# Reciprocals and products three to four slots later, room ahead of queries and post block, keys and scores at 112 columns

## What is computed

```python
# inputs: x (32, 56, 160), ctx_768 (32, 1500, 96); every weight is an input, fp32
def _L0_xattn_ref(hidden_states, encoder_hidden_states, w_q, w_k, w_v, w_k_dis, w_v_dis, w_out, b_out, n_heads):
    ...
    dis_tok = encoder_hidden_states[:, :N_AOE, :]
    anat_tok = encoder_hidden_states[:, N_AOE:N_AOE + N_IMG, :]
    delta_tok = encoder_hidden_states[:, -N_DELTA:, :]
    q = _heads(hidden_states @ w_q, n_heads)
    z_anat = _attend(q, _heads(anat_tok @ w_k, n_heads), _heads(anat_tok @ w_v, n_heads), scale)
    z_dis = _attend(q, _heads(dis_tok @ w_k_dis, n_heads), _heads(dis_tok @ w_v_dis, n_heads), scale)
    z_delta = _attend(q, _heads(delta_tok @ w_k_dis, n_heads), _heads(delta_tok @ w_v_dis, n_heads), scale)
    ...
    return out + residual

def cross_attention(x, ctx, wq, wk, wv, wo, bo):          # of L1: 20 heads of 64
    q = jnp.einsum('bne,ef->bnf', x, wq).reshape(B, N, HEADS, DHEAD).transpose(0, 2, 1, 3)
    k = jnp.einsum('bme,ef->bmf', ctx, wk).reshape(B, M, HEADS, DHEAD).transpose(0, 2, 1, 3)
    v = jnp.einsum('bme,ef->bmf', ctx, wv).reshape(B, M, HEADS, DHEAD).transpose(0, 2, 1, 3)
    scores = jnp.einsum('bhnd,bhmd->bhnm', q, k) * SCALE
    attn = jax.nn.softmax(scores, axis=-1)
    out = jnp.einsum('bhnm,bhmd->bhnd', attn, v)
    ...
    return jnp.einsum('bnf,fe->bne', out, wo) + bo

def block_forward(x, context, ...):                       # L1; L3 has the same form, 20 heads of 8
    x = cross_attention(layer_norm(x, g1, be1), layer_norm(x, g1, be1), wq1, wk1, wv1, wo1, bo1) + x
    x = cross_attention(layer_norm(x, g2, be2), context, wq2, wk2, wv2, wo2, bo2) + x
    return geglu_ff(layer_norm(x, g3, be3), w_ff1, b_ff1, w_ff2, b_ff2) + x

def _L2_xattn_ref(...):                                   # 8 heads of 20, last 4 context rows apart
    ...
    hs = _mha(query, keyt, valt)
    ca_hs1 = _mha(ca_q1, residual, residual)
    ...
    return out

x = _L0_xattn_ref(x, ctx_768, ...)
x = _L1_xattn_ref(x, ctx_768, ...)
x = _L2_xattn_ref(x, ctx_768, ...)
x = _L3_xattn_ref(x, ctx_768, ...)
```

## Time and profile before

| | us |
|---|---|
| median of 3 runs | 6163.31 (6159.48 to 6168.51) |
| the profiled execution, its own time | 6137.53 |
| its span in the profile | 6135.7 |
| TensorE busy | 5702.6 (93%) |
| TensorE weight loads busy | 4684.0 (76%) |
| VectorE busy | 2809.0 (46%) |
| ScalarE busy | 3107.8 (51%) |
| GpSimd busy | 3112.7 (51%) |
| mean granted clock of TensorE | 0.947 |

### The profile page before, as it was taken

How to read it: one execution, slowest core, us unless ns; L and a number is a source line. 1 busy time by engine, 2 the same in 40 slices (tenths; PEclk the granted TensorE clock), 3 DMA queues, 4 the chain that set the end, 5 groups by cost and what they waited for, 6 DMA issues and landing times.

```text
span 6135.7 us, 92602 instructions
## 1 busy us (share of the span) xinstructions
PE 5702.6 (93%) x34384; PEld 4684.0 (76%) x34384; DVE 2809.0 (46%) x5170; ACT 3107.8 (51%) x7280; POOL 3112.7 (51%) x3472
## 2 busy tenths in 40 slices
PE   7999999999999999988999999799999999999998
PEld 5777777778778877776666666588888878888887
DVE  1444444444444444434555555354444554444452
ACT  1445554545455545553445454256555555555554
POOL 0444444444444444463556555166555655555565
PEclk8899999999999999997899999599999999999998
DMA  2000000000000000000001011000000000000000
GB/s 55 12 16 16 16 13 15 16 16 15 16 15 12 13 16 11 16 20 19 27 24 32 25 29 41 8 19 16 18 16 15 20 18 19 16 15 18 15 19 10
DMA packets 84429, 114.48 MB, mean 19 GB/s; under 512 B 42814, under 2 KB 64682, under 8 KB 83978
## 3 DMA queue, kind: packets, MB, share of 16 engines
q1 hardware_dynamic: 83978, 108.56, 6.1%
HBM read 104.06 MB, written 4.46 MB: 18 GB/s over the span
## 4 chain that ended last, share of the span: by engine, by line
PE 68%; DVE 14%; ACT 8%; DMA 6%; issue 3%; POOL 2%; POOLq 0%; ACTq 0%; SPq 0%; DVEq 0%
PE ps_c L689 13%; PE ps_s L1128 6%; PE ps_c L1070 6%; PE ps_u L1143 5%; PE ps_s L1130 5%; PE ps_s L1129 5%; DVE mpiece L1452 5%; PE ps_u L1144 5%; PE ps_u L1145 5%; PE ps_c L1089 3%; ACT p L1819 2%; DMA w_area<-recs 2%; ACT p_hi L1821 2%; DMA sums<-uT 1%; DMA srec<-sums 1%
## 5 line engine op out<-in xcount | busy, mean ns | idle before, releaser
L1608 POOL TENSOR_TENSOR p_lo<-p,p_hi 125x448 fp32r<-125x448 f32 (+2 forms) x2688 | 2718.8, 1020 | 2292.3 <-ACT p_hi L1821 1626.0
L1819 ACT ACTIVATE p<-ps_s 125x448 f32<-125x448 f32 (+2 forms) x2688 | 1326.1, 493 | 2086.0 <-PE ps_s L1130 1903.5
L1821 ACT ACTIVATE p_hi<-ps_s 125x448 fp32r<-125x448 f32 (+2 forms) x2688 | 1316.0, 490 | 0.0
L1452 DVE TENSOR_REDUCE mpiece<-ps_c 125x1 f32<-125x500 f32 (+1 forms) x1984 | 1234.7, 668 | 105.2 <-PE ps_c L1070 98.2
L1128 PE MATMUL ps_s<-q_hi,ctxT_hi 105*125 105x448 f32 (+3 forms) x2688 | 1010.5, 376 | 38.1 <-ACT p_hi L1821 17.8
L1070 PE MATMUL ps_c<-ctxT_hi,q_hi 96*125 96x500 f32 (+1 forms) x2112 | 856.4, 432 | 132.6 <-DVE mpiece L1452 114.8
L1143 PE MATMUL ps_u<-p_hi,ctx_hi 125*97 125x448 f32 (+2 forms) x2688 | 975.9, 363 | 3.7 <-ACT uT L1809 2.7
L1129 PE MATMUL ps_s<-q_lo,ctxT_hi 96*125 96x448 f32 (+2 forms) x2688 | 934.8, 348 | 0.0
L1130 PE MATMUL ps_s<-q_hi,ctxT_lo 96*125 96x448 f32 (+2 forms) x2688 | 932.1, 347 | 0.0
L1144 PE MATMUL ps_u<-p_hi,ctx_lo 125*96 125x448 f32 (+2 forms) x2688 | 924.9, 344 | 0.0
L1145 PE MATMUL ps_u<-p_lo,ctx_hi 125*97 125x448 f32 (+2 forms) x2688 | 923.4, 344 | 0.0
(11 more groups left out here) (231 smaller groups left out, 6002.7 us busy)
## 6 DMA issues: line engine op xcount, KB each, us to landing
ctx_raw<-in_ctx SPq DMA_DIRECT2D x96, 562.5 KB
pT<-recs SPq DMA_DIRECT2D x32, 420.0 KB, 3.3
w_area<-recs SPq DMA_DIRECT2D x32, 420.0 KB, 3.2
w_area<-recs SPq DMA_DIRECT2D x32, 168.0 KB, 3.3
cs<-in_ctx SPq DMA_DIRECT2D x192, 6.0 KB, 3.0
x_between<-x_out SPq DMA_DIRECT2D x32, 80.0 KB
x_in<-x_between SPq DMA_DIRECT2D x32, 80.0 KB
w_area<-in_L_xattn_wq SPq DMA_DIRECT2D x2, 800.0 KB, 5.8
```

What stands on the lines that cost most here:

```text
L1452: z = V.tensor_reduce(mpiece[0:wide, k, r:r + 1], C(0, wide, n % banks(t), 0, PIECE), AX.X, ALU.max)
L1608: P.tensor_tensor(p_lo[0:kp, k % 3, 0:w], p32[0:kp, k % 2, 0:w], p_hi[0:kp, k % RING, 0:w].bitcast(F32), ALU.subtract).then_inc(*sig("pl_r ...
L1819: A(p32[0:kp, k % 2, 0:w], ps_s[0:kp, k % 2, 0:w], ACT.Exp, scale=DH[t.ph] ** -0.5)
L1821: A(p_hi[0:kp, k % RING, 0:w], ps_s[0:kp, k % 2, 0:w], ACT.Exp, scale=DH[t.ph] ** -0.5)\
```

## The change

It has four parts.

1. `normalise`: the reciprocals stand at slot 13 in place of 10. The products stand at POST-1 = 19 and then two slots apart (19, 21, 23), and four apart for b = 1 in phases 0 and 2 (19, 23, 27). In phase 1 there is one group of heads and one product, at 19. Before, they stood at 15, 16, 17.
2. `POST` is 20 in place of 16, so the second lane of phase 1 starts at slot 20 of 24. `TAIL` is 4 in place of 3. The `pre` laid ahead of a phase starts at slot 26 in place of 20.
3. `PARTS`: extra room ahead of `queries` (step 1) in all phases and ahead of `post` (step 1); and small extras in `pre` (steps 10, 27 and 30 in phase 0, step 13 in phase 2). As a half's slots stay as many, the other pieces move together.
4. In phase 0 the keys of the self attention (L862, L869) are computed at 2 x 56 columns in place of 2 x 64, as are its scores, and the two copies of the keys (VectorE L1301, ScalarE L1680) take 1120 columns in place of 1280. In phase 2 the scores (L1001) are computed at 56 columns a head. The queries keep their 64.

```diff
--- before.py
+++ after.py
@@ -391,13 +391,13 @@
 
 
         PARTS = {
-            "pre": ((40, 3, {4: 1, 7: 0.5, 8: 3, 10: 1, 14: 1.5, 16: 3, 18: 2, 22: 2, 27: 2, 30: 1, 34: 1, 35: 0.5, 37: 1,
-                             38: 1.5, 39: 2, 40: 4.5}), (29, 3.5, {5: 2, 15: 1.5, 22: 0.5, 23: 2}), (20, 2.5, {2: 3, 6: 1.5, 7: 0.5, 9: 2, 11: 0.5, 15: 1, 19: 2, 20: 1})),
-            "queries": ((7, 1, {7: 3}), (3, 3, {}), (7, 1, {7: 2})),
+            "pre": ((40, 3, {4: 1, 7: 0.5, 8: 3, 10: 1.5, 14: 1.5, 16: 3, 18: 2, 22: 2, 27: 2.5, 30: 1.5, 34: 1, 35: 0.5, 37: 1,
+                             38: 1.5, 39: 2, 40: 4.5}), (29, 3.5, {5: 2, 15: 1.5, 22: 0.5, 23: 2}), (20, 2.5, {2: 3, 6: 1.5, 7: 0.5, 9: 2, 11: 0.5, 13: 1, 15: 1, 19: 2, 20: 1})),
+            "queries": ((7, 1, {1: 2, 7: 3}), (3, 3, {1: 1}), (7, 1, {1: 2, 7: 2})),
             "split": ((4, 0.5, {}), (2, 0.5, {}), (4, 0.5, {})),
             "context": ((5, 1, {5: 6}), (4, 4, {}), (5, 1.5, {5: 3})),
             "maxima": ((31, 2.25, {}), (16, 3, {}), (31, 1.75, {})),
-            "post": ((15, 3, {6: 1, 14: 1}), (2, 1.5, {}), (15, 3, {6: 1.5})),
+            "post": ((15, 3, {1: 1, 6: 1, 14: 1}), (2, 1.5, {1: 1}), (15, 3, {1: 0.5, 6: 1.5})),
             "hand": ((1, 1, {}), (1, 1, {}), (1, 1, {})),
         }
 
@@ -405,8 +405,10 @@
         CUT = (18, 9, 3)
         LAST_NORM = (38, None, 18)
 
-        POST = 16
-        TAIL = 3
+        RECIP = 13
+        POST = 20
+        APART = (4, 2, 4)
+        TAIL = 4
 
         def schedule(eng, side, main):
 
@@ -528,7 +530,7 @@
                 elif not last:
                     lanes = [lane(before(t + 1, pre_b), 0.0, TAIL)]
                 elif t.ph < 2:
-                    lanes = [lane([part("pre", side.pre, At(t.ph + 1, 0, ahead=True))], POST + 4.0)]
+                    lanes = [lane([part("pre", side.pre, At(t.ph + 1, 0, ahead=True))], POST + 6.0)]
                 weave(main(t, 1, last=last), *lanes, apart(side.normalise(t, 0)))
 
             for ph in range(3):
@@ -857,8 +859,9 @@
                             if j == 0:
                                 pe.wait_ge(*(got("q_ready", t, 2) if w else got("ht_ready", t, 1)))
                                 pe.wait_ge(*late_loaded())
-                            z = both(C(0, 128, 0, 128 * j, 128), lambda i: l1_w[w][:, i, 128 * j:128 * j + 128],
-                                     lambda i: hT[:, i, :, :])
+                            each = slice(0, T if w else S)
+                            z = both(C(0, 128, 0, 128 * j, 128).rearrange("p (b s) -> p b s", b=2)[:, :, each],
+                                     lambda i: l1_w[w][:, i, 128 * j:128 * j + 128], lambda i: hT[:, i, :, each])
                         z.then_inc(*sig("qkv_psum"))
                     for b in range(2):
                         yield 24 + b
@@ -866,8 +869,8 @@
                             pe.wait_ge(*got("kb_ready", t, 2))
                             pe.wait_ge(*got("kb2_ready", t, 1))
                         for j in range(10):
-                            z = mm(C(S * b, S, 0, 128 * j, 128), qo3[:, j, S * b:S * b + S],
-                                   kb1[:, b, 2 * j:2 * j + 2, :], start=True, stop=True)
+                            z = mm(C(S * b, S, 0, 128 * j, 128).rearrange("p (e s) -> p e s", e=2)[:, :, 0:T],
+                                   qo3[:, j, S * b:S * b + S], kb1[:, b, 2 * j:2 * j + 2, 0:T], start=True, stop=True)
                     z.then_inc(*sig("s_psum"))
 
                     for b in range(2):
@@ -998,8 +1001,8 @@
                     pe.wait_ge(*got("vb_ready", t, 1))
                     for b in range(2):
                         for o, h0, h1 in ((0, 0, 8), (0, 8, 10), (1, 0, 6), (1, 6, 10)):
-                            z = mm(C(S * b, S, 0, 640 * o + S * h0, S * (h1 - h0)), q_small[:, o, b, :],
-                                   kb3[:, o, b, h0:h1, :], start=True, stop=True)
+                            z = mm(C(S * b, S, 0, 640 * o + S * h0, S * (h1 - h0)).rearrange("p (h s) -> p h s", s=S)[:, :, 0:T],
+                                   q_small[:, o, b, :], kb3[:, o, b, h0:h1, 0:T], start=True, stop=True)
                     z.then_inc(*sig("s_psum"))
                     yield 11
                     side.probs_T(t, 0, 10, 0)
@@ -1298,8 +1301,8 @@
                     side.norm(t, 0)
                     yield 23
                     dve.wait_ge(*got("qkv_psum", t, 3))
-                    V.tensor_copy(kb1[S:2 * S, :, 1::2, :].rearrange("p b j s -> p j b s"),
-                                  C(S, S, 0, 0, 1280).rearrange("p (j b s) -> p j b s", j=10, b=2))\
+                    V.tensor_copy(kb1[S:2 * S, :, 1::2, 0:T].rearrange("p b j s -> p j b s"),
+                                  C(S, S, 0, 0, 1280).rearrange("p (j b s) -> p j b s", j=10, b=2)[:, :, :, 0:T])\
                         .then_inc(*sig("kb_ready"))
                     yield 26
                     s = C(0, 128, 0, 0, 1280).rearrange("p (h w) -> p h w", h=20)[:, :, 0:T]
@@ -1468,11 +1471,11 @@
                 def normalise(t, b):
 
                     tiles = t.heads // 2
-                    yield 10
+                    yield RECIP
                     dve.wait_ge(*got("su_loaded", t, 16 * (b + 1)))
                     V.reciprocal(srec[:, 0:tiles], srec[:, 0:tiles]).then_inc(*sig("rec_ready"))
                     for g, (h0, n) in enumerate(t.groups):
-                        yield POST - 1 + g
+                        yield POST - 1 + (APART[t.ph] if b else 2) * g
                         if g == 0:
                             dve.wait_ge(*got("rb_loaded", t, 16 * (b + 1)))
                         u = uT[0:DC, h0:h0 + n, b, 0:T]
@@ -1677,8 +1680,8 @@
                         A(qo[:, :], side_banks(t)(0, 128, 0, 0, 1280), ACT.Copy).then_inc(*sig("q_ready"))
                         yield 23
                         act.wait_ge(*got("qkv_psum", t, 3))
-                        A(kb1[0:S, :, 0::2, :].rearrange("p b j s -> p j b s"),
-                          side_banks(t)(0, S, 0, 0, 1280).rearrange("p (j b s) -> p j b s", j=10, b=2), ACT.Copy)\
+                        A(kb1[0:S, :, 0::2, 0:T].rearrange("p b j s -> p j b s"),
+                          side_banks(t)(0, S, 0, 0, 1280).rearrange("p (j b s) -> p j b s", j=10, b=2)[:, :, :, 0:T], ACT.Copy)\
                             .then_inc(*sig("kb2_ready"))
                         yield 27
                         side.exps(t, 1, smv[:, :, 0:T])
```

## The result

The changed kernel took 5991.75 us (median of 4 runs, 5981.94 to 6001.57) against 6161.4 us before (4 runs), ratio 0.973, 95% interval 0.9702 to 0.9759. The prediction was 6067 us with a range of 5990 to 6135: the direction held, the range held by 1.75 us, the size did not. Forecast were 96 us off; 170 came off by the medians, 147 by the two profiled executions (spans 6135.7 and 5989.0). Two later jobs gave the changed kernel 0.977 (0.9744 to 0.9796) and 0.9768 (0.9738 to 0.9798), that is 138 and 140 us off.

A forecast was written before the change was run, and what follows sets the result against it. TensorE, busy 91% to 95%, bounds the kernel. Phases 0, 2, 1, phase 1's clock and the phase change sum -39 -72 -3 +15 +3 = -96 us, 6137.5 to 6041; 25.8 carried over gives 6067, 80% range 5990 to 6135.

The forecast's parts named there:

- The stretch in phase 2: Phase 2, reciprocals to negated maxima: 23.45 us shrinks to 19.7 (bounds 19.1 and 21.5) as VectorE's DMA waits shrink.
- Maxima stretch, phase 0: Phase 0 maxima, VectorE the bound: both its DMA-related waits go, -2.4 us a pair; squeezing adds +0.2 and +0.4.
- Post block: Phase 0 post block's 1.04 us wait for the row of maxima: 0.7 taken away; clock behind it gives 0.6.
- The clock: TensorE's granted clock, per pair: phase 0 gains 0.6 us, phase 2 somewhat over 1, phase 1 loses 1.
- Columns: Phase 0 scores -0.6 us a pair, keys zero since the weight load sets the pace; phase 2 scores -0.4.
- One step earlier, one step later: Phase 0, per pair: probabilities' transposes a group earlier, +0.6 us; values' copy behind later products, +0.5; queries' norm wait unchanged.
- Phase 1: Phase 1, per pair: crowded post lane +0.7 us, queries' room -0.9, net -0.2; denser idle time costs +1 in clock.
- rival (d): Clock comes back everywhere: phase 0 keeps 1.1 us a pair, phase 1 -45, phase 2 another 10; 5985 us, chance 0.11.
- Rival (a): Phase 1 gives much back, every pair at 68.10 us and beyond, +45 to +60 us; 6110 us, chance 0.12.
- (c): VectorE also bounds phase 2, or its wait only moves: first product still holds reductions, -1.5 a pair; 6115 us, chance 0.10.
- Rival (b): Slower: phase 1's crowded four slots keep the lower clock, 8 us or more a pair; at 9, 6190 us; chance 0.07.
- Rival (e): Phase 0 keys gain from fewer columns as the scores do, 0.6 us times 16; 6057 us, chance 0.05.

The follow-up runs named there:

- room_only: Kernel before with all of the changed PARTS (extra room) and TAIL 4, nothing else; 6157.54 us, ratio 1.005.
- late_only: Kernel before with only reciprocals, products, POST and the lane laid ahead moved as in the change; 6035.55 us, ratio 0.9848.
- best1: Changed kernel with four shifts: pre step 8, post step 6 and queries later, maxima of phase 1's first half earlier; 5963.85 us, ratio 0.9757.
- late_cols: Changed kernel with the old PARTS and TAIL 3, so without the extra room; 6020.37 us, ratio 0.9822.
- best2: Changed kernel with phase 0's pre, post and queries shifts, smaller phase 2 queries shift, later phase 0 self attention outputs, phase 1 unshifted; 5951.16 us, ratio 0.9718.
- cols_only: Kernel before with only keys, their copies and scores at 112 columns, order of phase 1 untouched; 6114.04 us, ratio 0.998.

## Why the prediction was right, and where it was short

*The mechanism.* Right, and shown by taking it away: with the products early the gain is gone (0.9987), and with the reciprocals alone early phase 0 gives back 2.3 of its 3.1 us a pair. The stretch in phase 2 came out at 19.67 us for 19.7. The reciprocals' own wait went in phase 0 (26.9 to 0.5 us in 13 pairs); in phase 2, where I had none left, 0.8 us a pair stayed (14.1 to 11.4 in 14).

*Where the size was missed.* Of the 51 us by which the profiled execution beats my sum, phase 1 has 24, the stretches outside the steady pairs 13, phase 2 has 8 and phase 0 has 6. The 24 of phase 1 are its spread and a clock term that did not come; the clock term of phases 0 and 2 was too small by some 30 us, and other terms there took half of that back.

*Maxima stretch, phase 0.* The net forecast was -1.8 us a pair; the waits for the reductions fell by 1.35 (50.4 to 30.1 over 15). I wrote that the total would be under 15 us, which does not follow from my own sum; VectorE remains the bound there. Its casts also got slower where they now stand (402 to 622 ns in the mean), its long products faster (1004 to 707). I had both at the length that they had before. The trace shows what goes with it, GpSimd:

```profile
1313.51 1.16 POOL L1611 TENSOR_TENSOR p_lo<-p,p_hi 125x448 fp32r<-125x448 f32 x1
...
1317.73 0.61 DVE L1482 TENSOR_TENSOR uT<-uT,pT 96x448 f32<-96x448 f32 x1
...
1321.69 0.66 POOL L1611 TENSOR_TENSOR p_lo<-p,p_hi 125x224 fp32r<-125x224 f32 x1 [0.30 <-ACT p_hi L1824]
1321.78 1.04 DVE L1482 TENSOR_TENSOR uT<-uT,pT 96x448 f32<-96x448 f32 x1
```

In the steady pairs of phase 0 a 96x448 product that starts with no GpSimd instruction under way takes 0.61 to 0.62 us. One that starts beside one ends 0.48 us behind the end of the GpSimd instruction, in all 26 such cases before and all 11 after. The cast of 1.33 us at 1313.55 stands likewise beside the `p_lo` at 1313.51 and ends 0.21 us behind it. 39 of 78 casts had a GpSimd instruction under way at their start before, 76 of 78 after, 13 of which now take 1.3 us. Of the 37 waits for reductions that are left, 26 (21.3 us) come behind a cast and 11 (5.1 us) behind a product. No run varied this.

*Post block.* Forecast -0.7 of 1.04 us; it went whole. Another wait of 0.7 us behind the norm of the same block (L1099, 9.6 us in 14) came, which I did not look for. The room does it: room_only has this wait (8.9 us in 13), late_only does not. best1 removed it.

*The clock.* This is the term that was mis-sized. I took 0.6 us a pair in phase 0 from the one row of the post block, and "somewhat over 1" in phase 2. TensorE's busy time in the steady pairs fell by 33 us in 13 pairs and 34 in 14, that is 2.5 us a pair each. The scores' fewer columns are 0.5 of it in either phase (L872: 62.3 to 55.4 us; L1004's four shapes: 79.6 to 72.1). So 2.0 and 1.9 us a pair are clock. The bound that I should have used stood in the trace: 95.6 us at half clock in 13 pairs is at most 3.7 us a pair.

The same record says where the falls are. For each stretch at half clock I took the longest of TensorE's waits just ahead of it (number of stretches, their us):

| steady pairs | phase 0: reductions | post block | copy of the values | phase 2: reductions | value products |
|---|---|---|---|---|---|
| before | 13 (65) | 9 (31) | | 14 (72) | 6 (20) |
| late_only | | 7 (24) | | | 7 (24) |
| room_only | 16 (68) | | 3 (31) | 14 (89) | |
| late_cols | | 5 (27) | | | 4 (14) |
| changed | 2 (7) | | | | |

In phase 0 I had priced the falls behind the post block and put those behind the reductions, twice as many us, at nothing. Late reciprocals and products take away the falls behind the reductions; the room takes away those behind the two short waits; it takes both parts of the change for the whole clock. The rows show, of the kernel before, a wait for a reduction and the stretch behind it (columns as in the earlier trace rows; the granted clock is third from the end), and then the same of late_only's value products:

```profile
4381.01 0.78 PE L1070 MATMUL ps_c<-ctxT_hi,q_hi 96*125 96x500 f32 x1 [2.83 <-DVE mpiece L1452]
4381.02:4384.43 3.41, 3.41 (x9) 2.81 (x10) 3.38 (x7) 0.98 (x2) 0.57 (x1) 0.50 0.02 7
...
4255.15 2.30 PE L768 MATMUL ps_c<-vb_s,pT 128*64 128x16 f32 x40 [0.69 <-ACT pT L1737]
4257.95:4261.30 3.35, 3.35 (x11) 2.66 (x10) 0.69 (x2) 1.58 (x4) 1.14 (x1) 0.50 0.00 0
```

Neither the sum of the waits nor the longest one tells the falls by itself. late_cols waits 6.6 us a pair in phase 0 with 27 us at half clock, the changed kernel 6.9 with 7. The falls in phase 2 of late_only come behind 0.7 us, while the queries' wait of 1.0 us for the norm, which every kernel but best1 and best2 has, has no fall of phases 0 and 2 behind it. The projection now takes 5.64 or 5.65 us in every steady pair of phase 0, in place of 7.32 in nine:

```profile
362.75 5.65 PE ps_c L1092 x40
...
2456.59 5.64 PE ps_c L1092 x40
```

*Columns.* Right: keys 2.40 to 2.39 us a run of 20, scores 2.40 to 2.13, and -0.5 a pair for phase 2's.

*One step earlier, one step later.* Right: L759 waits 0.6 us more (5.4 in 14 to 14.0 in 14), the copy of the probabilities 0.6 (0.5 forecast), the queries' wait unchanged. Not forecast: the wait for `sm` at L689 (10.7 us) went with the room.

*Phase 1.* The waits' sum was right by luck of opposite errors. Per pair all waits went from 5.5 to 5.2 us, forecast -0.2. The first scores wait 0.85 us longer, as forecast (0.8), the key blocks 0.8 (up to 1.3 forecast), the reductions and the queries less; the transposes of the new rows were to be longer and are shorter (18.4 to 4.4 us in 14 pairs). room_only alone shows that (4.3 us); late_only has 10.8, so the later slots did not lengthen them either. The +1 us a pair for the clock did not come: with the old order 109 us at half clock before and 66 in cols_only, with the new one 116, 85 and 102 in three profiles of the changed kernel. Nothing here shows that the order moved it; the falls only come behind other waits (the reductions before, the first scores after). best1, with 17.8 us of waits for the exponentials, has 137.

*The carry-over.* I added the 25.8 us by which the profiled execution of before lay under its median. The changed kernel's profiled execution lies 1 us from its median. The same kernel before gave medians of 6161, 6130, 6121, 6113 and 6124 us in five jobs, and runs from 6102 to 6169; the changed kernel's stay within 30 us over three jobs. Part of the miss (147 of span against 170 of medians) is that unsteadiness: in the two later jobs the change was worth 138 and 140 us. That the unsteadiness comes from the falls of the clock is likely, since it went with them, but was not tested.

*The rivals.* The time landed near rival (d)'s 5985 (its own terms add up to some 5990), but not by its way: phases 0 and 2 got all of their clock back, which is more than it had, and phase 1, where it had most, got none. Rival (a) is out, since phase 1 gave nothing back, and so is (c), since the first product has no wait and the stretch its forecast length. Rival (b) has no trace: no steady pair of phase 1 exceeds 66 us. Rival (e) is out by the keys' 2.39 us.

## What to carry over

Where a short ring of banks couples two engines, ask what the engine that empties it stands at: here a DMA wait placed inside the stretch came back as a longer stretch and as clock (2.3 us a pair for 2.1), while such a wait ahead of the stretch cost little (0.4 for 1.4). Price the clock from the time at half clock over the whole phase, not from one block that happens to show it, and read which wait each fall stands behind. Take the spread of a phase from a kernel that leaves its order alone, before a small difference is explained. When an instruction moves, look at what the other engines do where it goes. And count the slots on both sides of a wait that is left: one more group of matmuls ahead of it takes it away, unless the lane has no slack to give.

## What was not expected of the hardware

TensorE's clock was granted whole through all of phase 2 (0 of 1813 us at half) once the reductions' waits of up to 3.7 us and the value products' 0.7 us were both gone, with the queries' wait of 1.0 us still there; with the 3.6 us wait back, 79 us were at half clock. With the value products' wait alone left, seven pairs of 14 had a fall behind it (late_only, 24 us).

VectorE's product of 96x448 took 0.61 us or 1.04 us in one stretch of the changed kernel's phase 0, its cast of 125x384 took 0.59 and 1.33 us. The product of 1.04 us and the cast of 1.33 us run beside a GpSimd instruction nearly from its start and end 0.47 and 0.21 us behind its end; that the GpSimd instruction is the cause was read from the order of time and not tested by a run.
